# Seven products of quarters in place of eight for M = (I + W0)(I + W1), in a fused chain of four conditional layers

## What is computed

```
x = x + (x W0^T + b0) + scale[e0] * (x A0[e0]^T) B0[e0]^T        # e0 per batch, 8 adapters, rank 16
x = x + (x W1^T + b1) + (x A1[e1]^T) B1[e1]^T                    # e1 per batch, 32 adapters, rank 16
x = x + x W2[e2]^T                                               # e2 per batch, 8 matrices
x = x + W3[e3]^T x                                               # e3 per batch, 16 matrices of 64x64, over the 64 rows
```

## Time and profile before

| | us |
|---|---|
| median of 3 runs | 576.79 (576.33 to 577.38) |
| the profiled execution | 577.23 |
| its span, first to last instruction | 575.3 |
| TensorE busy in the span | 568.5 |
| VectorE, ScalarE, GpSimd busy | 281.2, 246.5, 56.0 |
| main part of pair 0 starts | 156.66 |

### The profile page before, as it was taken

One profiled execution on the slowest core, in us unless ns is written; L12 is line 12 of the kernel. 1 busy time (PEld: TensorE's weight loads), 2 busy tenths in 40 slices (PEclk: granted clock), 3 DMA queues, 4 the chain that ended last, 5 costly groups with the idle time before them and its releaser, 6 DMA issues.

```text
span 575.3 us, 10398 instructions
## 1 busy us (share of the span) xinstructions
PE 568.5 (99%) x2706; PEld 476.4 (83%) x2707; DVE 281.2 (49%) x520; ACT 246.5 (43%) x308; POOL 56.0 (10%) x87
## 2 busy tenths in 40 slices
PE   8999999999999999999999999999999989999997
PEld 7888888888888888888888888888888878888885
DVE  5986211122666367733435674333568349633210
ACT  5633211115643439435352844435365538353201
...
PEclk9999999999999999999999999999999999999999
...
DMA packets 66301, 60.92 MB, mean 106 GB/s; under 512 B 42082, under 2 KB 50402, under 8 KB 66276
## 3 DMA queue, kind: packets, MB, share of 16 engines
...
...
## 4 chain that ended last, share of the span: by engine, by line
PE 99%; DVE 0%; issue 0%; ACT 0%; POOL 0%; POOLq 0%
PE y_ps L1276 31%; PE y_ps L1311 28%; PE y_ps L1226 11%; PE t_ps L1226 6%; PE t_ps L1303 5%; PE low_ps L1266 3%; PE y_ps L1339 3%; PE y_ps L1207 3%; PE y_ps L1198 1%; PE y_ps L1292 1%; PE y_ps L1291 1%; PE low_ps L1207 1%; PE t_ps L1207 1%; PE y_ps L1325 1%; PE t_ps L1217 1%; PE y_ps L1155 1%
## 5 line engine op out<-in xcount | busy, mean ns | idle before, releaser
L1276 PE MATMUL y_ps<-wm,ops 128*128 128x512 f32 x768 | 179.7, 391 | 0.0
L1276 PEld LDWEIGHTS y_ps<-wm,ops 128*128 128x128 f32 x768 | 141.9, 188 | 28.9
L1311 PE MATMUL y_ps<-ring,ops 128*128 128x512 f32 x696 | 164.4, 392 | 0.0
L1311 PEld LDWEIGHTS y_ps<-ring,ops 128*128 128x128 f32 x696 | 129.7, 188 | 26.8
L597 ACT CAST ops<-arena 128x512 fp32r<-128x512 f32 x32 | 19.7, 620 | 91.9 <-PE y_ps L1276 91.9
L1226 PE MATMUL y_ps<-ring,wm 128*128 128x512 f32 x240 | 55.3, 390 | 0.0
L1014 DVE TENSOR_TENSOR ops<-t_ps,ops 128x512 fp32r<-128x512 f32 x32 | 22.1, 690 | 63.1 <-ACT ops L650 53.6
L1226 PEld LDWEIGHTS y_ps<-ring,wm 128*128 128x128 f32 x240 | 44.9, 188 | 9.3
L650 ACT CAST ops<-t_ps 128x512 fp32r<-128x512 f32 x32 | 18.7, 589 | 78.0 <-PE t_ps L1303 77.6
L1002 DVE TENSOR_TENSOR ring<-arena,ring 128x1024 fp32r<-128x1024 f32 x40 | 48.4, 1246 | 5.6 <-ACT ring L628 4.9
L495 POOL TENSOR_TENSOR w_stage<-w_stage,ident 128x128 f32<-128x128 f32 x16 | 11.8, 736 | 370.5 <-DMA w_stage<-w 370.5
...
## 6 DMA issues: line engine op xcount, KB each, us to landing
...
arena<-xt SPq DMA_DIRECT2D x32, 256.0 KB, 2.8
out<-arena SPq DMA_DIRECT2D x30, 256.0 KB, 3.1
a_stage<-a_tab SPq DMA_DIRECT2D x64, 64.0 KB, 1.8
arena<-b_tab SPq DMA_DIRECT2D x64, 64.0 KB, 2.0
...
arena<-a_cols SPq DMA_DIRECT2D x8, 256.0 KB, 4.0
a_tab<-bias SPq DMA_DIRECT2D x4, 256.0 KB, 8.4
```

Source lines behind the costliest of these rows:

```text
L1276: op = nc.tensor.matmul(main_ps(j)[:, cols], xs[:, k, part_x, :], wm[:, k, part_w, cols], start=k == 0 and part_x == part_w, stop=False)
L1311: op = nc.tensor.matmul(y[:, cols], xs2[:, k, part_x, :], ring[:, k, part_w, cols], start=k == 0 and part_x == part_w, stop=k == KT - 1 an ...
```

## The change

The core of the diff, with the calls of an order joined in one line by semicolons; the functions that it names are the sums, casts and low parts told above:

```diff
-        a1_tab = nc.dram_tensor("a1_tab", [N_LORA1, P, KT * RANK], F32).ap()
+        a1_tab = nc.dram_tensor("a1_tab", [P, KT, N_LORA1, RANK], F32).ap()
+PAIR_OF = (0, 1, 2, 0, 1, 2, 0, 1, 2, 0, 1, 2, 0, 2)
+FIRST_S, FIRST_T, SECOND_T, SECOND_S = 0, 4, 8, 10
 # SP
+            sp.wait_ge(acc_w_step, KT - 2)
+            load_w0(0, 0, BANK)
+            store_a1(range(2))
+            sp.wait_ge(acc_w_step, KT - 1)
+            load_w0(1, 1, BANK)
+            store_a1(range(2, 4))
+            sp.wait_ge(acc_w_step, KT)
+            load_w0(2, 2, BANK)
+            store_a1(range(4, KT))
+            sp.wait_ge(s2_lo, 1)
+            load_w0(3, 3, BANK)
+            sp.wait_ge(evictions, KT + 1)
+            sp.dma_start(g_tab.rearrange("e r n -> (e r) n"), evicted(KT)).then_inc(g_stored, 16)
+            sp.wait_ge(s2_lo, 2)
+            load_w1(4, (0, HK))
+            sp.wait_ge(s2_lo, 3)
+            load_w1(5, (1, HK + 1))
...
+            sp.wait_ge(s2_lo, 4)
+            load_w1(6, (2, HK + 2))
+            sp.wait_ge(t4_lo, 1)
+            load_w1(7, (3, HK + 3))
+            sp.wait_ge(t4_lo, 2)
+            load_w1(8, (0, 1))
+            sp.wait_ge(t4_lo, 3)
+            load_w1(9, (2, 3))
+            load_w3(0)
+            sp.wait_ge(t4_lo, 4)
+            load_w0(10, 0)
+            sp.wait_ge(t1_lo, 2)
+            load_w0(11, 1)
+            sp.wait_ge(t1_lo, 4)
+            load_w0(12, 2)
+            sp.wait_ge(bias_ready, 2)
+            sp.dma_start(d_tab.rearrange("e r o -> o (e r)"), d_row).then_inc(d_stored, 16)
+            sp.wait_ge(s1_lo, 2)
+            load_w0(13, 3)
...
+            load_a(which)
+            sp.wait_ge(s1_lo, HK)
+            load_b(which)
+            first_matrix(range(2))
+            sp.wait_ge(m21_lo, HK)
+            first_matrix(range(2, HK))
+            sp.wait_ge(m22_lo, 2)
+            load_x(0)
...
+            sp.wait_ge(m12_lo, HK)
+            first_matrix(range(HK, KT))
 # GpSimd, one tile k of W0
+                fold_block(qa21[:, k * P:(k + 1) * P]).then_inc(s_folded, 1)
+                pool.wait_ge(s_folded, k + 1)
+                nc.gpsimd.tensor_tensor(qa22, qa21, qa22, ALU.add).then_inc(s1_sum, 1)
+                nc.gpsimd.tensor_tensor(qa21, qa11, qa21, ALU.subtract).then_inc(s3_sum, 1)
+                pool.wait_ge(s1_sum, k + 1)
+                nc.gpsimd.tensor_tensor(qa11, qa22, qa11, ALU.subtract).then_inc(s2_sum, 1)
+            for k in range(3): first_s(k)
+            fold_t(0)
+            first_s(3)
+            for k in range(1, HK): fold_t(k)
+            fold_t1(SECOND_T); fold_t1(SECOND_T + 1)
+            fold_w3(0)
+            for k in range(HK): second_s(k)
 # ScalarE, start of its order
+            for n in range(KT): evict(n)
+            s3_hi_part(0); evict(KT); s2_hi_part(0)
+            for k in range(1, 3): s3_hi_part(k); s2_hi_part(k)
+            acc_w_hi(); take_b0(); first_t_hi(0); s3_hi_part(3); s2_hi_part(3)
+            keep_m1(0); keep_m1(1); first_t_hi(1); keep_m1(2); keep_m1(3)
+            t4_hi_part(0); t4_hi_part(1); first_t_hi(2); t4_hi_part(2)
+            m11_hi_part(0); m11_hi_part(1); first_t_hi(3); t4_hi_part(3); m11_hi_part(2); m11_hi_part(3)
...
 # VectorE, start of its order
+            s3_lo_part(0); s2_lo_part(0); order_the_batches()
+            for k in range(1, 3): s3_lo_part(k); s2_lo_part(k)
+            t_sums(0); rank_the_matrices(); first_t_lo(0); s3_lo_part(3); s2_lo_part(3); acc_w_lo()
+            t_sums(1); first_t_lo(1); plan_layer2(); t_sums(2); t4_lo_part(0); t4_lo_part(1)
+            first_t_lo(2); t4_lo_part(2); m11_lo_part(0); m11_lo_part(1)
+            t_sums(3); first_t_lo(3); t4_lo_part(3); m11_lo_part(2); m11_lo_part(3)
+            for k in range(HK): t1_sum_again(k)
+            for k in range(HK): t1_lo_part(k)
+            add_s3_t3(0); add_s3_t3(1); acc_a_lo(); s4_lo_part(0); add_s3_t3(2); add_s3_t3(3)
+            s4_lo_part(1); s1_lo_part(0); s1_lo_part(1); add_s2_t2(0); add_s2_t2(1)
+            s4_lo_part(2); s1_lo_part(2); add_s2_t2(2); add_s2_t2(3); s4_lo_part(3); s1_lo_part(3)
+            sum_m21(0); a_lo(0); sum_m21(1)
...
 # TensorE
+            def quarter_product(to, left, right, i, left_lo=None, right_lo=None, adds=False, goes_on=False):
+                for k in range(HK):
+                    if i == 0 and left_lo: pe.wait_ge(left_lo, k + 1)
+                    if i == 0 and right_lo: pe.wait_ge(right_lo, k + 1)
+                    for part_l, part_r in SPLIT:
+                        op = nc.tensor.matmul(to, left[:, i, part_l, k * P:(k + 1) * P], right[:, k, part_r, :],
+                                              start=not adds and k == 0 and part_l == part_r,
+                                              stop=not goes_on and k == HK - 1 and part_l == 1, skip_group_check=True)
+                op.then_inc(product_done, 1)
+            def s3_t3(i):
+                if i < 2: pe.wait_ge(m11_lo, i + 3)
+                else: pe.wait_ge(m2_ready, i - 1)
...
+            def a22_t4(i):
+                if i < 2: pe.wait_ge(m2_ready, i + 3)
+                else: pe.wait_ge(m21_sum, i - 1)
...
+            same_products()
+            b0_products()
             place_products()
+            a11_b11(0); a11_b11(1)
             rank_products()
+            a11_b11(2); a11_b11(3)
+            for i in range(HK): a12_b21(i)
             bias_products()
+            for i in range(HK): s3_t3(i)
             d_products()
+            for i in range(HK): s2_t2(i)
+            for i in range(HK): a22_t4(i)
+            for i in range(HK): s1_t1(i)
+            for i in range(HK): s4_b22(i)
 # TensorE, first_step, ahead of main_part(0, 0)
+                pe.wait_ge(m12_sum, HK)
+                pe.wait_ge(m21_lo, HK)
+                pe.wait_ge(m22_lo, HK)
```

537 lines of the change are left out of this document (436 added, 101 removed).

## The result

The changed kernel takes 599.18 us (median of 4 runs, 597.71 to 599.94) against 577.09 (576.33 to 578.23) for the kernel before beside it: a ratio of 1.038, 95% interval 1.035 to 1.041. The forecast was 579.5, in a range that ended at 585.0. The profiled execution's span is 597.2 us, 21.9 more than before's 575.3.

The account below looks back on a forecast made before the run. TensorE, busy for 99% of the span, was taken as the bound; 10.88 us saved against 14.2 of new waits put the main part 2.75 us later: 577.23 + 2.75 - 0.44 = 579.5 us, range 570.5 to 585.

Parts of the forecast that it names:

- 48 matmuls, 10.88 us less: Forming M on TensorE: 336 matmuls instead of 384, in 28 blocks of 2.72 us, 10.88 us saved.
- The places and releasers of the five waits: TensorE gaps before the order's first products, rank products, S3 T3, A22 T4's third block and main part: 14.2 us with rounding.
- The last wait, X + 57.7, 1.3 us: Before pair 0's main part: TensorE asks at X + 56.4, M12's last sum comes at X + 57.7 behind two remainders.
- X: End of M11's third remainder, before which S3 T3 can't start: 95.4 us without contention, 100.2 with it.
- The clock: Rival: TensorE's clock falls behind the 2.7 and 5.5 us waits, one block costs 2.7 us more: 582.2 us; chance 0.12.
- Contention: GpSimd and VectorE taking turns at SBUF: 0.8 us a meeting, six ahead of X (+4.8), two behind (+1.5).
- few meetings: Rival: the chain without 6.3 us of GpSimd-VectorE contention, 573.3 us, from 571.5 to 577; chance 0.29.
- Up to 57 us: Start of the stage: fourth A1 table store lands at 56.6, eviction ends at 57.2, TensorE waits 2.3 us.
- The sum itself: Whole path: main part starts 2.75 us later; waits of 14.2 against 10.88 saved called the same but for rounding.
- A22 T4's third block: Its sum on VectorE stands behind S1's last remainder, ready at X + 28.5, asked at X + 28.25; wait 1.8 with contention.
- A1's gather at nothing: Loading A1's table in 64-byte pieces: hidden, so no cost; uncovered 0.7 us a pair.
- The size of the room: From 54 to 156 us VectorE is busy for 25.3 of 102 us, ScalarE 28.4, GpSimd 4.6, taken as room for added work.

Follow-up runs that it names:

- e1_end: Changed kernel with M12's sums freed of the ring's remainders on VectorE and ScalarE's casts reordered to fit: 591.52 us, ratio 1.025.
- e5_gaps: Kernel before with three waits of TensorE put between M's blocks, behind 1, 3 and 8 ScalarE copies: 592.57 us (one run).
- e6_order: Changed kernel with the products and steps of the order of the batches moved later on TensorE and VectorE: 597.74 us.
- e3_fill: Changed kernel with small unused matmuls of the identity filling TensorE's five waits: 597.16 us.
- e2_m21: Changed kernel with M21's first two sums ahead of the last remainders of S4 and S1 on VectorE: 601.29 us.
- e4_table: Kernel before with A1's table laid out by partition and nothing else: 577.85 us against 577.82, ratio 1.0004.
- e15_oldtab: Changed kernel with the old layout of A1's table (by adapter) put back alone: 612.49 us.
- e17b_x1both: e16b_x1's edits on e11_sums plus the last sums of T ahead of layer 2's plan and the bias, bias and d products later: 583.01 us.
- e16b_x1: e11_sums with pair 0's low sums and layer-2 x earlier, and pair 1's x ahead of the ring's last four tiles: 583.10 us.
- e11_sums: Changed kernel with e1_end's, e2_m21's and e6_order's edits, S3 T3's other banks, B's parts behind M22's, M12's sums first: 583.12 us, ratio 1.010.

## Why the prediction was wrong

- *48 matmuls, 10.88 us less*: right, to the 2.72 us a block.
- *The places and releasers of the five waits*: right. Their sum was 14.2 and is 20.6.
- *Where the 15.3 us lie*: main_part was to start at 159.4 and starts at 174.7. S3 T3 starts 4.4 late; from there to A22 T4's third block it is 33.1 us for 30.0, 3.1 more; from there to main_part 36.9 for 29.2, 7.7 more. The time is another 3.9 over my sum for what lies behind.
- *The last wait, X + 57.7, 1.3 us*: the step that failed most. I put "a remainder of the ring (1.2) and one of M12" ahead of the last sum, and read VectorE's order alone. With ScalarE's order beside it the four sums form a ring of 4.06 us a round: 6.9 us, and with the slow matmuls behind it 7.7 us of time (e1_end). A part of it is the start: x, which I had among what costs nothing, made ScalarE wait until 158.5, and VectorE's order has its remainders ahead of the first sum, which starts at 161.75.
- *The clock*: a rival with 0.12, and priced for one block. It falls at all five waits, and not at 1.17 (e5_gaps), 1.5 or 3.28 us (e6_order). Its price a time, 1.75 to 2.9 us, was near my 2.7; and I was right that what runs slow ahead of a wait is covered by it (e3_fill: 2.0 us in all). But I charged it behind the wait of S3 T3, where later waits cover it too, and put nothing behind the last wait, which has no cover. So the clock was worth 2 us. The Trainium skill (TensorE: Matmul & The Clock Gate, section The HAM clock gate) says that idleness brings half rate back; the windows at 0.50 agree, and a rival with 0.12 was too little for it.
- *Contention*: six meetings at 0.8, 4.8 us, ahead of X. The rows show 0.9 for S3's first remainder, 2.9 for three small steps and 3.4 for T's first four sums, 7.2 us. Behind X I had 1.5: there two remainders of S1, which let the last pair of W0 load, took 3.5 us for 1.3, and five of nine sums on GpSimd 1.6 to 1.7 for 1.3, some 4 us together in the chain that was 3.1 late. The mechanism was right; it was under-sized, and small instructions had no price. The rival *few meetings* was wrong.
- *Up to 57 us*: the order's first products start at 59.45, not 57.2; the first wait is 4.6 for 2.3. I counted 2.62 MB up to the fourth store. The queues moved 3.1 MB from 48 to 58 us (311 GB/s), for the loads of the third pair, issued from 53.15, ran beside that store; and two issues of SP took 1.1 us each there, which I took at nothing. Which of the two held the store isn't separated. The chain is late by the same amount (S2's first remainder ends at 63.7 for 61.2), and with the meetings that makes S3 T3's 104.64 for 100.2.
- *The sum itself*: my waits of 14.2 less 10.88 make 3.3, not the 2.75 that the path gave, and by the working's own times the third wait was 100.2 - 94.1 = 6.1, not 5.5. That is more than rounding, though small beside the miss.
- *A22 T4's third block*: the wait is 3.55 for 1.8. Taken away alone it is worth nothing (e2_m21).
- *A1's gather at nothing*: right for the time of the kernel before (e4_table). ScalarE's waits grew more than the 0.7 a pair; the 1.4 us behind main_part are there without the gather too (e15_oldtab).
- *The size of the room*: I read 25.3 of 102 us of VectorE as free space and then followed one path. The whole work added to it, 38.5 us in the changed kernel between 55 and 184, was never summed against what TensorE waits for. In the reordered versions I hold it responsible for the last 5.7 us, which is argued above and not shown; the cause of these stays open.

No version beats the kernel before. The best, e17b_x1both, e16b_x1 and e11_sums at 583.0 to 583.1, are 1.0% slower. Of the 22 us lost, the orders on ScalarE, VectorE and TensorE, with S3 T3's other banks, gave back 16. Open is whether the rest yields to an order not tried, such as a part of the first matrix of layer 2 converted ahead of M22, or the low sums of pair 1 and B's parts both ahead of the ring's last four tiles; and how much of it is A1's gather.

## What to carry to other kernels

Taking matmuls from a saturated TensorE pays only if the sums, casts and reloads that replace them fit on the other engines, per stage and added up over every engine, with their meetings. Read two engines' orders side by side where each waits for the other: here a ring of casts and remainders cost 4.06 us per block, and it is seen only in both. Where the engines that feed TensorE are late by themselves, as here, an early wait is covered by a later one and only the last, with the half-clock matmuls behind it, is time (e1_end against e2_m21 and e6_order); where nothing is late behind them, all of them are (e5_gaps). So take waits away from the end, and expect each to come back at the next place where the same chain is asked for.

## What the runs showed of the chip

- A wait of 1.17 us left TensorE's clock up, and so did one of 3.28 us (e6_order). Behind each of the five of 2.21 to 6.86 us in the changed kernel it was 0.50 for a while, and the matmuls there took 1.75 to 2.55 us more, whether 24 or 48 stood in the block; behind 6.17 us in e5_gaps it was 2.9. Small matmuls in the waits kept it at 1.00 (e3_fill).
- Beside a GpSimd instruction with its data in SBUF, a VectorE instruction on 32x33 numbers took 1.21 us instead of 0.17: it ended within 0.04 us of GpSimd's.
- SP's issue of a load of 512 KB, 0.33 us, took 2.95 behind stores in pieces of 64 bytes; two such stores took 5.65 us, two in rows of 2 KB 0.90.
